# Last sums of the expert outputs: five pairs of tiles on TensorE, three on VectorE, none on GpSimd

## The chip, the cores and the metric

The kernel runs on one core of a Trainium2 chip. The metric is the device time of one execution in microseconds (us). Before the change it was 656.49 us, the median of three runs (655.33 to 656.53).

## What is computed

One transformer layer on 2 x 1024 tokens of width 256, in float32: a modulated layer norm, causal attention with 16 heads, a gated residual, a second modulated layer norm, and a mixture of 16 experts with a shared expert, gated and added to the residual. Only the end matters here. Cut to it, the reference is

```python
w, eidx = jax.lax.top_k(masked, K)            # K = 4 experts of each token
w = w / (w.sum(-1, keepdims=True) + 1e-20)
for e in range(E):                            # cw[:, e] is w where e was chosen, else 0
    a = _swiglu(xt @ expert_up_w[e].T)
    out = out + cw[:, e:e + 1] * (a @ expert_down_w[e].T)
out = out + _swiglu(xt @ shared_up_w.T) @ shared_down_w.T
x = x + gb * out                              # gb: one row for each of the two sequences
```

So each token has four expert outputs. They are weighted with four numbers of the token, summed, multiplied with the row `gb` and added to `x`.

## The kernel before

The 2048 tokens are 16 tiles of 128 (`NT`), one token in each SBUF partition. `X` holds the residual stream, [128, 16, 256].

Attention fills the span up to about 430 us, then the shared expert runs, and from about 460 us on the expert blocks. There are `NB` = 79 blocks of 128 token rows. For a block, SyncE loads the rows into `G`; TensorE turns them (L2376), multiplies with the expert's up weights (L2422), turns the activations (L2434) and multiplies with the down weights (L2446 to L2451); ScalarE and VectorE do the splits in a high and a low part and the SwiGLU between these steps; ScalarE copies the result to `Y` (L1458); GpSimd scatters `Y` to the DRAM tensor `expert_rows` (L1248), so that the four outputs of a token lie beside each other. One step of this loop takes about 2 us.

ScalarE has one more piece of work in this loop. `make_diagonal(i)` (L1466) writes a 128 x 128 diagonal matrix into `DG`, with the weights of one tile's tokens for one of their four experts on the diagonal. It makes one in each step from step `DIAG_FROM` = 12 on, 32 in all.

The expert weights lie in SBUF in 18 slots (`W`, slot k at `k * EW`). Slots 0 and 1 hold the shared expert (`NSH` = 2), slot 2 the first expert. When their contents are no longer needed, the slots are used again: `DG` begins at slot 0, and `Z`, the place for the expert outputs, at slot 2.

When the last needed scatter has landed, the end begins. SyncE issues 16 loads `Z[:, t]` of 512 KB each (L680), one for a tile, and after them, on the same queue, the stores of `X` to `out` (L1030), by pairs of tiles in `STORE_ORDER`. Each of the eight pairs of tiles is summed in one of two ways:

- A pair of `PE_PAIRS`: for each tile TensorE multiplies the four `DG` matrices with the four parts of `Z` and adds them up in PSUM (L2469, `add_outputs`; the trace has eight matrix instructions for a tile). Then VectorE multiplies the sums with the gate row (L2003) and adds them to `X` (L2005): `finish`. The last pair, 7, is finished tile by tile, which halves the size of these instructions.
- Any other pair: ScalarE scales the eight parts of `Z` in place (L1473, `scale_outputs`). Then VectorE or GpSimd does four elementwise instructions, `add_pair`: an addition of 1024 elements in a partition (L723), one of 512 (L725), the product with the gate row (L727) and the addition to `X` (L729). All their operands are in SBUF, while L2003 reads its sums from PSUM.

The division is a constant:

```python
PE_PAIRS, POOL_PAIRS, DVE_PAIRS = (1, 3, 5, 7), (0, 4), (2, 6)
```

Every engine takes its pairs in rising order; VectorE takes 1, 2, 3, 5, 6 and 7. GpSimd's two pairs come after its last scatter.

Of the kernel before, what the change touches and what calls it, by code (L numbers as in the profile page):

```python
# [5 lines left out]
F32 = mybir.dt.float32  # L6
# [5 lines left out]
ALU = mybir.AluOpType  # L12
# [3 lines left out]
P = 128  # L16
B, S, H = 2, 1024, 256
NH, HD = 16, 16
T = B * S
KH = H // P  # L20
NT = T // P
CH = 512
NC = T // CH
# [12 lines left out]
NGR, TOPG, TOPK = 4, 2, 4  # L36
# [9 lines left out]
EW = 2 * HIW + H  # L46
RAW = HIW + H

NSH = 2
# [6 lines left out]
NW = NSH + NE  # L56
# [243 lines left out]
PLACE = [0, 1, 2, 3, 4, 5, 6, 13, 16, 17, 7, 14, 15, 8, 9, 10, 11, 12]  # L300
# [12 lines left out]
COUNT_AT = 8  # L313


PE_PAIRS, POOL_PAIRS, DVE_PAIRS = (1, 3, 5, 7), (0, 4), (2, 6)
SCALED = sorted(POOL_PAIRS + DVE_PAIRS)
LAST_PAIR = NT // 2 - 1
assert LAST_PAIR in PE_PAIRS and sorted(PE_PAIRS + POOL_PAIRS + DVE_PAIRS) == list(range(NT // 2))
ADD_STEPS = 4  # L320

STORE_ORDER = (1, 2, 0, 3, 5, 4, 6, 7)
DIAG_FROM = 12
SP_LOAD, SP_AHEAD = 4, 6


# [3 lines left out]
def program(nc, x, wqk, bqk, wv, bv, wout, bout, cT, wmod, wgate, wsh, wexp, qkd, modrows, hTd, xd, padd, zd, wd, out):  # L330
    with ExitStack() as ctx:

        def sem(name):
            return ctx.enter_context(nc.semaphore(name))
# [19 lines left out]
        X = keep.put("X", [P, NT, H], F32)  # L354
# [33 lines left out]
        att0 = BASE + KEEP + ROWSZ  # L388
# [69 lines left out]
        hv = under.put("hv", [P, KH, CH], F32)  # L458
        SBr = under.put("SBr", [P, B, H], F32)
        CBr = under.put("CBr", [P, B, H], F32)  # L460
        Z = nc.alloc_sbuf_tensor_at("Z", [P, NT, TOPK, H], F32, offset=att0 + NSH * EW * 4)
        assert NSH * EW + NT * TOPK * H <= PLACE[NW - 1] * EW

        DG = nc.alloc_sbuf_tensor_at("DG", [P, 2 * len(PE_PAIRS), TOPK, P], F32, offset=att0)
        assert 2 * len(PE_PAIRS) * TOPK * P <= NSH * EW

        late = Area(att0 + NW * EW * 4, early0 + EARLY - att0 - NW * EW * 4)

# [72 lines left out]
        modrow_in = sem("modrow_in")  # L541
# [96 lines left out]
        x_add = sem("x_add")  # L638
        diag_done = sem("diag_done")
        z_scaled = sem("z_scaled")  # L640
        z_ps = sem("z_ps")
        z_step = sem("z_step")
        z_pool = sem("z_pool")
        fin_done = sem("fin_done")
        out_done = sem("out_done")

# [31 lines left out]
        def load_outputs(queue, t):  # L678

            queue.dma_start(Z[:, t, :, :], zd[t * P * TOPK:(t + 1) * P * TOPK, :].rearrange("(p j) h -> p j h", j=TOPK)  # L680
                            ).then_inc(z_in[t], 16)
# [17 lines left out]
        def pad_experts(queue, which, lo, hi):  # L699

            queue.wait_ge(prow_ready, 1)
            queue.wait_ge(pad_kept, 16 * 4)
            _, first = nc.values_load_multi_w_load_instructions(
                prow[0:1, lo:hi], engines=(which,), min_val=0, max_val=NE * STR - P,
                skip_runtime_bounds_check_because="an expert's stretch has room for every token and the rows behind")
            for e in range(lo, hi):
                queue.dma_start(xd[bass.ds(first[e - lo], P), :], padd[e]).then_inc(pad_out, 16)

        def sums_of(i, first, n):

            if PE_PAIRS[i] == LAST_PAIR:
                return allb[i + first][:, 0:H].unsqueeze(1)
            return allb[i][:, first * H:(first + n) * H].rearrange("p (t h) -> p t h", h=H)

        def gate_of(k):

            return GBr[:, 2 * k // (NT // B), :].unsqueeze(1).broadcast_to([P, 2, H])

        def add_pair(eng, ops, step, i, k):

            z, two = Z[:, 2 * k:2 * k + 2, :, :], slice(2 * k, 2 * k + 2)
            eng.wait_ge(z_scaled, SCALED.index(k) + 1)
            ops.tensor_tensor(z[:, :, 0:2, :], z[:, :, 0:2, :], z[:, :, 2:4, :], ALU.add).then_inc(step, 1)  # L723
            eng.wait_ge(step, ADD_STEPS * i + 1)
            ops.tensor_tensor(z[:, :, 0, :], z[:, :, 0, :], z[:, :, 1, :], ALU.add).then_inc(step, 1)  # L725
            eng.wait_ge(step, ADD_STEPS * i + 2)
            ops.tensor_tensor(z[:, :, 0, :], z[:, :, 0, :], gate_of(k), ALU.mult).then_inc(step, 1)  # L727
            eng.wait_ge(step, ADD_STEPS * i + 3)
            ops.tensor_tensor(X[:, two, :], X[:, two, :], z[:, :, 0, :], ALU.add).then_inc(step, 1)  # L729

        def low_part(eng, ops, c):

# [43 lines left out]
        def _(sp):  # L776
# [240 lines left out]
                sp.wait_ge(y_sc[i], sends[i])  # L1017
            for t in range(NT):
                load_outputs(sp, t)
            for k in STORE_ORDER:  # L1020
                if k in POOL_PAIRS:
                    sp.wait_ge(z_pool, ADD_STEPS * (POOL_PAIRS.index(k) + 1))
                elif k in DVE_PAIRS:
                    sp.wait_ge(z_step, ADD_STEPS * (DVE_PAIRS.index(k) + 1))

                tiles = [(2 * k, 2)] if k != LAST_PAIR else [(2 * k, 1), (2 * k + 1, 1)]
                for t, n in tiles:
                    if k in PE_PAIRS:
                        sp.wait_ge(fin_done, PE_PAIRS.index(k) + 1 + t % 2)
                    sp.dma_start(out[t * P:(t + n) * P, :].rearrange("(t p) h -> p t h", p=P),  # L1030
                                 X[:, t:t + n, :]).then_inc(out_done, 16)
# [6 lines left out]
        def _(pool):  # L1038
# [33 lines left out]
            for k in range(tiles + 1):  # L1072
                if k < tiles:
                    c, i, m = S // CH + k // 4, k % 4, M_ORDER[k % 4]
# [169 lines left out]
            def scatter_block(b):  # L1244

                pool.wait_ge(y_read, b + 1)
                pool.wait_ge(yix_step, 2 * b + 2)
                nc.gpsimd.indirect_dma_start(  # L1248
                    out=zd, out_offset=bass.IndirectOffsetOnAxis(ap=YIX[:, b:b + 1], axis=0),
                    in_=Y[b % YRING], in_offset=None).then_inc(y_sc[b % YRING], 16)  # L1250

            for s in range(NB + 2):
                if s >= 2:
                    scatter_block(s - 2)
            pool.wait_ge(modrow_in, 48)
            pool.wait_ge(x_add, 2 * NC)
            for i, k in enumerate(POOL_PAIRS):
                add_pair(pool, nc.gpsimd, z_pool, i, k)

# [1 line left out]
        def _(act):  # L1263
# [187 lines left out]
            def copy_block(u):  # L1451
                act.wait_ge(y_ps, u + 1)
                if u >= YRING:
                    act.wait_ge(y_sc[u % YRING], 16 * (u // YRING))
                elif u % 2 == 0:

                    act.wait_ge(x_add, 2 * NC - 1 + u // 2)
                nc.scalar.activation(Y[u % YRING], ybank[:, 0:H], ACT.Copy).then_inc(y_read, 1)  # L1458

            def make_diagonal(i):  # L1460

                t, j = 2 * PE_PAIRS[i // (2 * TOPK)] + i // TOPK % 2, i % TOPK
                if i == 0:
                    act.wait_ge(s_down, 2 * NC)
                    act.wait_ge(route_step, NC * ROUTE_STEPS)
                nc.scalar.activation(DG[:, i // TOPK, j, :], ident[:, :], ACT.Identity,  # L1466
                                     scale=W4[:, t, j:j + 1]).then_inc(diag_done, 1)

            def scale_outputs(t):

                act.wait_ge(z_in[t], z_count(t))
                for j in range(TOPK):
                    ins = nc.scalar.activation(Z[:, t, j, :], Z[:, t, j, :], ACT.Identity, scale=W4[:, t, j:j + 1])  # L1473
                return ins

            for s in range(-2, NB + 2):
# [6 lines left out]
                if s >= 2:  # L1483
                    copy_block(s - 2)
                if 0 <= s - DIAG_FROM < 2 * len(PE_PAIRS) * TOPK:
                    make_diagonal(s - DIAG_FROM)
            for k in SCALED:
                for t in (2 * k, 2 * k + 1):
                    ins = scale_outputs(t)
                ins.then_inc(z_scaled, 1)  # L1490
# [3 lines left out]
        def _(dve):  # L1494
# [496 lines left out]
            def act_low(u):  # L1991
                dve.wait_ge(ah_done, u + 1)
                if u >= 2:
                    dve.wait_ge(y_ps, u - 1)
                nc.vector.tensor_tensor(al[u % 2][:, :], abank[:, 0:2 * P], ah[u % 2][:, :].bitcast(F32),
                                        ALU.subtract).then_inc(al_done, 1)

            def finish(i, first, n):

                k = PE_PAIRS[i]  # L2000
                t = slice(2 * k + first, 2 * k + first + n)
                dve.wait_ge(z_ps, 2 * i + first + n)
                nc.vector.tensor_tensor(Z[:, t, 0, :], sums_of(i, first, n), gate_of(k)[:, 0:n, :], ALU.mult).then_inc(s_gated, 1)  # L2003
                dve.wait_ge(s_gated, 2 * NC + i + first + 1)
                nc.vector.tensor_tensor(X[:, t, :], X[:, t, :], Z[:, t, 0, :], ALU.add).then_inc(fin_done, 1)  # L2005

# [10 lines left out]
                    count_sends()  # L2017
            for k in range(NT // 2):
                if k in DVE_PAIRS:
                    add_pair(dve, nc.vector, z_step, DVE_PAIRS.index(k), k)  # L2020
                if k in PE_PAIRS and k != LAST_PAIR:
                    finish(PE_PAIRS.index(k), 0, 2)
            for first in range(2):
                finish(PE_PAIRS.index(LAST_PAIR), first, 1)

        @block.tensor
        def _(pe):
# [435 lines left out]
            def add_outputs(i, u):  # L2463
# [4 lines left out]
                for j in range(TOPK):  # L2468
                    ins = nc.tensor.matmul(sums_of(i, u, 1)[:, 0, :], DG[:, 2 * i + u, j, :], Z[:, t, j, :],  # L2469
                                           start=(j == 0), stop=(j == TOPK - 1))  # L2470
# [64 lines left out]
```

## Time and profile before

| | |
|---|---|
| median of three runs | 656.49 us |
| the profiled execution: device time | 657.58 us |
| the profiled execution: span of the trace | 655.5 us |
| TensorE busy | 583.3 us (89%) |
| VectorE busy | 493.2 us (75%) |
| ScalarE busy | 384.0 us (59%) |
| GpSimd busy | 354.3 us (54%) |
| first load of Z issued | 616.25 us |
| last matrix instruction ends | 645.19 us |
| last instruction of VectorE ends | 650.91 us |

Times in the trace are counted from the start of the span. PE is TensorE, DVE VectorE, ACT ScalarE, POOL GpSimd, SP SyncE; SPq is SyncE's queue of DMA issues. A row of a timeline gives start, duration, engine, line, operation, output and inputs, and in brackets how long the engine was idle before and what it waited for. Between the last instruction of VectorE and the end of the span lie the last store and the end of the program.

### The profile page before, as it was taken

To read this page: it belongs to the slowest core of one execution; us is meant where nothing else is said; L and a number is where in the kernel's file an instruction comes from. 1 tells how busy PE (TensorE), PEld (TensorE's weight loads), DVE (VectorE), ACT (ScalarE), POOL (GpSimd) and SP (SyncE) were. 2 spreads that over 40 slices of the span, in tenths; PEclk is the share of its full clock that TensorE was granted. 3 is DMA by queue.
4 is the path that set the end of the run, shared out by engine and by line. 5 is a ranking of instruction groups with operands and counts; after the bars stand their busy time and mean duration, and the time that the engine had idled before them with its cause. 6 is when DMAs were issued, how large, how long until landed. Compare 5 with 4: busy or idle time off the path is not lost. (4 is left out here: it accounts for less than half of the span.)

```text
span 655.5 us, 13633 instructions
## 1 busy us (share of the span) xinstructions
PE 583.3 (89%) x3944; PEld 394.8 (60%) x3944; DVE 493.2 (75%) x1409; ACT 384.0 (59%) x926; POOL 354.3 (54%) x593
## 2 busy tenths in 40 slices
PE   3979889999999999998987699995999999999972
PEld 3767433434343443444332288774899999999962
DVE  4888978888888769777948657886767777666667
ACT  4547337666667656655857453543367777666671
POOL 5515514455757536854648876772144444444474
PEclk9989969999999999998989989999899999999997
DMA  8359956861707263542215143686954444444594
GB/s 277 125 179 285 350 169 180 209 204 73 233 6 234 86 195 131 168 176 69 82 49 179 51 171 106 232 256 233 342 172 132 134 138 138 133 134 133 187 409 175
DMA packets 69066, 113.62 MB, mean 173 GB/s; under 512 B 12578, under 2 KB 51106, under 8 KB 67844
## 3 DMA queue, kind: packets, MB, share of 16 engines
q1 hardware_dynamic: 62036, 93.74, 44.6%
q0 software_dynamic: 6864, 19.01, 7.5%
q8 instruction: 34, 0.56, 0.4%
q14 instruction: 36, 0.29, 0.1%
q10 hardware_dynamic: 96, 0.01, 0.0%
HBM read 60.57 MB, written 49.94 MB: 169 GB/s over the span
## 5 line engine op out<-in xcount | busy, mean ns | idle before, releaser
L1396 ACT ACTIVATE Pr<-bank 128x512 f32<-128x512 f32 (+3 forms) x384 | 165.8, 494 | 98.3 <-PE bank L2173 93.9
L1248 POOL DMA_INDIRECT expert_rows<-Y,YIX x79 | 75.7, 959 | 104.4 <-DVE ytmp L1957 74.5
L1536 DVE TENSOR_REDUCE mxA<-bank 128x1 f32<-128x128 f32 (+3 forms) x256 | 112.3, 483 | 25.0 <-PE bank L2069 24.8
L2173 PE MATMUL bank<-Qs,Ks 99*128 99x512 bf16 (+3 forms) x384 | 119.5, 336 | 7.4 <-ACT Pr L1396 3.8
L2069 PE MATMUL bank<-Ks,Qs 96*128 96x512 bf16 (+3 forms) x384 | 122.7, 336 | 1.9 <-DVE mxA L1536 1.3
L1536 DVE TENSOR_REDUCE mxB<-bank 128x1 f32<-128x512 f32 x128 | 81.5, 680 | 13.6 <-PE bank L2069 13.6
L2159 PE MATMUL bank<-Pr,Vst 128*32 128x512 f32 (+3 forms) x768 | 84.0, 510 | 5.5 <-POOL Pr L1232 5.3
L1182 POOL DMA_INDIRECT chosen_rows<-Hx,pos x64 | 70.5, 1101 | 22.1 <-issue 17.5
L1230 POOL TENSOR_TENSOR tick<-ident 128x1 f32<-128x1 f32 x128 | 25.3, 198 | 101.5 <-ACT Pr L1396 100.8
L2422 PE MATMUL bank<-W,xh 128*128 x316 | 78.7, 331 | 0.6 <-issue 0.6
L2173 PEld LDWEIGHTS bank<-Qs,Ks 99*128 99x128 bf16 x384 | 36.0, 99 | 61.3 <-ACT Pr L1396 36.6
L2067 PE MATMUL bank<-mask,identb 128*128 128x128 bf16 x256 | 55.3, 228 | 7.6 <-DVE mxA L1536 5.3
L1987 DVE TENSOR_TENSOR act_a<-bank,sg 128x176 f32<-128x176 f32 x79 | 27.0, 341 | 45.8 <-ACT sg L1443 45.8
L2069 PEld LDWEIGHTS bank<-Ks,Qs 96*128 96x128 bf16 x384 | 38.2, 100 | 28.9 <-DVE mxA L1536 5.7
L1232 POOL TENSOR_SCALAR_AFFINE_SELECT Pr<-Pr 128x256 f32<-128x256 f32 x128 | 54.1, 422 | 0.0
L2422 PEld LDWEIGHTS bank<-W,xh 128*128 128x128 f32 x316 | 52.5, 190 | 1.4 <-issue 1.0
L2422 PE MATMUL bank<-W,xl 128*128 x158 | 51.5, 326 | 0.0
L1443 ACT ACTIVATE sg<-bank 128x176 f32<-128x176 f32 x79 | 25.1, 317 | 40.3 <-PE bank L2422 40.3
L2067 PEld LDWEIGHTS bank<-mask,identb 128*128 128x128 bf16 x256 | 25.2, 99 | 30.3 <-DVE mxA L1536 13.8
L1458 ACT ACTIVATE Y<-bank 128x256 f32<-128x256 f32 x79 | 30.4, 384 | 13.8 <-PE bank L2451 4.8
L1950 DVE TENSOR_TENSOR xl<-bank,xh 128x256 fp32r<-128x256 f32 x79 | 32.7, 413 | 5.9 <-ACT xh L1437 5.9
L2376 PE MATMUL bank<-ident,G 128*128 128x128 f32 x158 | 30.9, 278 | 5.4 <-DMA G<-chosen_rows 5.4
(258 smaller groups left out, 1333.0 us busy)
## 6 DMA issues: line engine op xcount, KB each, us to landing
G<-chosen_rows SPq DMA_DIRECT2D x79, 132.0 KB
Z<-expert_rows SPq DMA_DIRECT2D x16, 512.0 KB, 13.5
W<-expert_words SPq DMA_DIRECT2D x7, 1088.0 KB, 6.9
qk_parts<-AP SPq DMA_DIRECT2D x16, 384.0 KB, 5.2
Qs<-qk_parts SPq DMA_DIRECT2D x16, 384.0 KB, 4.6
Ks<-qk_parts SPq DMA_DIRECT2D x8, 768.0 KB, 9.1
Wraw<-in_wexp SPq DMA_DIRECT2D x9, 608.0 KB, 5.7
SA<-in_wexp SPq DMA_DIRECT2D x7, 608.0 KB, 10.8
```

What stands on the lines that cost most here:

```text
L1182: nc.gpsimd.indirect_dma_start(out=xd, out_offset=bass.IndirectOffsetOnAxis(ap=pos[:, c * TPC + t, j:j + 1], axis=0), in_=chosen(c)[:, t, ...
L1232: nc.gpsimd.affine_select(out=v, in_=v, compare_op=ALU.is_ge, fill=0.0, base=0, pattern=[[0, 2], [1, P]], channel_multiplier=-1).then_inc( ...
L1248: nc.gpsimd.indirect_dma_start(out=zd, out_offset=bass.IndirectOffsetOnAxis(ap=YIX[:, b:b + 1], axis=0), in_=Y[b % YRING], in_offset=None) ...
L1396: nc.scalar.activation(Pr[(2 * s + j // 2) % 4][:, j % 2, 0:w], ebank[p % RING][:, 0:w], ACT.Exp, scale=SCALE).then_inc(exp_done, EXP)
L1536: nc.vector.tensor_reduce(dst, mbank[u % RING][:, 0:w], AX.X, ALU.max).then_inc(m_red, 1)
L1950: nc.vector.tensor_tensor(xl[u % 2][:, :], xbank[:, 0:H], xh[u % 2][:, :].bitcast(F32), ALU.subtract).then_inc(xl_done, 1)
L2067: nc.tensor.matmul(mbank[u % RING][:, w - P:w], identb[:, :], mask[:, :], start=True, stop=False, skip_group_check=True)
L2069: nc.tensor.matmul(mbank[u % RING][:, 0:w], Qs[slot][0:NPR, i // TPC, j, (i % TPC) * P:(i % TPC + 1) * P], Ks[slot][0:NPR, j, k0:k0 + w], ...
L2159: ins = nc.tensor.matmul(pvb[32 * j:32 * j + 32, q0:CH], Vst[slot][:, kt, 32 * j:32 * j + 32], Pr[(2 * s + j // 2) % 4][:, j % 2, 0:w], st ...
L2173: nc.tensor.matmul(ebank[p % RING][:, 0:CH - q0], Ks[slot][0:NAUG, j, kt * P:(kt + 1) * P], Qs[slot][0:NAUG, qc, j, q0:CH], start=True, st ...
L2376: ins = nc.tensor.transpose(xbank[:, k * P:(k + 1) * P], G[u % GRING][:, k * P:(k + 1) * P], ident[:, :])
L2422: ins = nc.tensor.matmul(ubank[u % 2][:, 0:2 * EI], x_part[u % 2][:, k * P:(k + 1) * P], words(u, first + k * 2 * EI, 2 * EI), start=(k == ...
```

## The change

GpSimd's two pairs go away. TensorE takes the pairs 0, 2, 4, 6 and 7, VectorE 1, 3 and 5. The stores are issued in rising order. There are 40 diagonals instead of 32; `DG` grows into the slot of the first expert, so `Z` begins one slot later, and the first diagonal is made in step 20, so that the first expert's at most 16 blocks are done before a diagonal is written into its slot. ScalarE scales three pairs instead of four. `add_pair` has the same four instructions, on VectorE alone.

```diff
-PE_PAIRS, POOL_PAIRS, DVE_PAIRS = (1, 3, 5, 7), (0, 4), (2, 6)
-SCALED = sorted(POOL_PAIRS + DVE_PAIRS)
+PE_PAIRS, DVE_PAIRS = (0, 2, 4, 6, 7), (1, 3, 5)
...
-STORE_ORDER = (1, 2, 0, 3, 5, 4, 6, 7)
-DIAG_FROM = 12
+DIAG_FROM = 20
+assert DIAG_FROM >= T // P + 2
...
-        Z = nc.alloc_sbuf_tensor_at("Z", [P, NT, TOPK, H], F32, offset=att0 + NSH * EW * 4)
+        Z = nc.alloc_sbuf_tensor_at("Z", [P, NT, TOPK, H], F32, offset=att0 + (NSH + 1) * EW * 4)
...
-        assert 2 * len(PE_PAIRS) * TOPK * P <= NSH * EW
+        assert 2 * len(PE_PAIRS) * TOPK * P <= (NSH + 1) * EW and PLACE[NSH] == NSH
...
-            for k in STORE_ORDER:
-                if k in POOL_PAIRS:
-                    sp.wait_ge(z_pool, ADD_STEPS * (POOL_PAIRS.index(k) + 1))
-                elif k in DVE_PAIRS:
+            for k in range(NT // 2):
+                if k in DVE_PAIRS:
                     sp.wait_ge(z_step, ADD_STEPS * (DVE_PAIRS.index(k) + 1))
...
-            pool.wait_ge(modrow_in, 48)
-            pool.wait_ge(x_add, 2 * NC)
-            for i, k in enumerate(POOL_PAIRS):
-                add_pair(pool, nc.gpsimd, z_pool, i, k)
...
-            for k in SCALED:
+            for k in DVE_PAIRS:
                 for t in (2 * k, 2 * k + 1):
                     ins = scale_outputs(t)
                 ins.then_inc(z_scaled, 1)
```

## Rows read from the trace of the kernel before

**Rows 1.** The page: busy time of each engine, share and instructions

```profile
PE 583.3 (89%) x3944; PEld 394.8 (60%) x3944; DVE 493.2 (75%) x1409; ACT 384.0 (59%) x926; POOL 354.3 (54%) x593
```

**Rows 2.** The chain that ended last: start, duration, engine and line

```profile
627.01 6.38 ACT Z L1473 x16
633.42 2.07 DVE Z L723
...
650.49 0.42 DVE X L2005
```

**Rows 3.** Timeline of VectorE at the end

```profile
629.75 0.69 DVE L2003 TENSOR_TENSOR Z<-bank,GBr 128x512 f32<-128x512 f32 x1 [4.82 <-PE bank L2469]
...
635.51 1.64 DVE L725 TENSOR_TENSOR Z<-Z 128x512 f32<-128x512 f32 x1
...
643.20 0.68 DVE L2003 TENSOR_TENSOR Z<-bank,GBr 128x512 f32<-128x512 f32 x1
643.91 1.05 DVE L2005 TENSOR_TENSOR X<-X,Z 128x512 f32<-128x512 f32 x1
644.88 2.28 DVE L723 TENSOR_TENSOR Z<-Z 128x1024 f32<-128x1024 f32 x1
647.19 0.69 DVE L725 TENSOR_TENSOR Z<-Z 128x512 f32<-128x512 f32 x1
...
649.25 0.41 DVE L2003 TENSOR_TENSOR Z<-bank,GBr 128x256 f32<-128x256 f32 x1
...
650.04 0.42 DVE L2003 TENSOR_TENSOR Z<-bank,GBr 128x256 f32<-128x256 f32 x1
```

**Rows 4.** Timeline of GpSimd in the same stretch

```profile
634.47 2.13 POOL L727 TENSOR_TENSOR Z<-Z,GBr 128x512 f32<-128x512 f32 x1
...
642.80 1.60 POOL L727 TENSOR_TENSOR Z<-Z,GBr 128x512 f32<-128x512 f32 x1
644.48 1.59 POOL L729 TENSOR_TENSOR X<-X,Z 128x512 f32<-128x512 f32 x1
```

**Rows 5.** VectorE groups by form: count, busy us, mean ns

```profile
L1852 DVE TENSOR_TENSOR SX<-SX,XH 128x1024 fp32r<-128x1024 f32 x4 | 4.9, 1214 | 0.3 <-ACT XH L1363 0.3
```

**Rows 6.** Timeline of TensorE at the end

```profile
626.10 3.62 PE L2469 MATMUL bank<-Z,DG 128*128 128x256 f32 x16
631.24 3.72 PE L2469 MATMUL bank<-Z,DG 128*128 128x256 f32 x16 [1.53 <-DMA Z<-expert_rows]
...
641.47 3.72 PE L2469 MATMUL bank<-Z,DG 128*128 128x256 f32 x16 [1.22 <-DMA Z<-expert_rows]
```

**Rows 7.** Timeline of ScalarE at the end

```profile
634.02 3.30 ACT L1473 ACTIVATE Z<-Z,W 128x256 f32<-128x256 f32 x8 [0.64 <-DMA Z<-expert_rows]
638.97 3.30 ACT L1473 ACTIVATE Z<-Z,W 128x256 f32<-128x256 f32 x8 [1.65 <-DMA Z<-expert_rows]
```

**Rows 8.** Stretches: us, busy PE, PEld, DVE, ACT, POOL, granted clock, DMA share, GB/s

```profile
540.00:550.00 10.00, 10.00 (x77) 9.90 (x76) 6.93 (x31) 7.67 (x26) 4.71 (x6) 1.00 0.43 136
560.00:570.00 10.00, 10.00 (x76) 9.80 (x75) 6.87 (x30) 6.08 (x21) 4.26 (x6) 1.00 0.43 133
```

**Rows 9.** The instructions that write DG: duration min/median/max ns, first and last start

```profile
L1466 ACT ACTIVATE DG<-ident,W x32: 392/392/395, 490.3 to 552.8; 128x128 f32<-128x128 f32 x32
```

**Rows 10.** Store issues from 633 to 634 us: count, KB, us to landing

```profile
out<-X SPq DMA_DIRECT2D x1, 256.0 KB, 10.1
```

**Rows 11.** DMA from 641.0 to 655.5 us: GB/s in 40 slices; last stores

```profile
GB/s 381 206 68 20 260 342 350 345 209 345 333 23 0 175 347 201 138 356 229 0 0 0 0 0 0 147 347 328 263 57 302 3 0 0 0 0 0 0 0 0
...
out<-X SPq DMA_DIRECT2D x2, 128.0 KB, 1.7
```

**Rows 12.** Stretches, columns of Rows 8: a stretch with low clock, the end

```profile
456.00:463.00 7.00, 5.24 (x19) 4.75 (x20) 2.75 (x8) 0.77 (x2) 0.00 (x0) 0.53 0.93 351
...
636.00:641.00 5.00, 3.72 (x16) 2.96 (x16) 4.93 (x3) 3.35 (x10) 4.92 (x3) 1.00 1.02 416
```

**Rows 13.** Timeline of TensorE where the clock is low

```profile
457.76 0.69 PE L2376 MATMUL bank<-ident,G 128*128 128x128 f32 x2 [4.76 <-DMA G<-chosen_rows]
```

More of the change, by code:

```diff
@@ L313 @@
 COUNT_AT = 8
-PE_PAIRS, POOL_PAIRS, DVE_PAIRS = (1, 3, 5, 7), (0, 4), (2, 6)
-SCALED = sorted(POOL_PAIRS + DVE_PAIRS)
+PE_PAIRS, DVE_PAIRS = (0, 2, 4, 6, 7), (1, 3, 5)
 LAST_PAIR = NT // 2 - 1
-assert LAST_PAIR in PE_PAIRS and sorted(PE_PAIRS + POOL_PAIRS + DVE_PAIRS) == list(range(NT // 2))
+assert LAST_PAIR in PE_PAIRS and sorted(PE_PAIRS + DVE_PAIRS) == list(range(NT // 2))
 ADD_STEPS = 4
-STORE_ORDER = (1, 2, 0, 3, 5, 4, 6, 7)
-DIAG_FROM = 12
+DIAG_FROM = 20
+assert DIAG_FROM >= T // P + 2
 SP_LOAD, SP_AHEAD = 4, 6
@@ L460, in program @@
         CBr = under.put("CBr", [P, B, H], F32)
-        Z = nc.alloc_sbuf_tensor_at("Z", [P, NT, TOPK, H], F32, offset=att0 + NSH * EW * 4)
-        assert NSH * EW + NT * TOPK * H <= PLACE[NW - 1] * EW
+        Z = nc.alloc_sbuf_tensor_at("Z", [P, NT, TOPK, H], F32, offset=att0 + (NSH + 1) * EW * 4)
+        assert (NSH + 1) * EW + NT * TOPK * H <= PLACE[NW - 1] * EW
         DG = nc.alloc_sbuf_tensor_at("DG", [P, 2 * len(PE_PAIRS), TOPK, P], F32, offset=att0)
-        assert 2 * len(PE_PAIRS) * TOPK * P <= NSH * EW
+        assert 2 * len(PE_PAIRS) * TOPK * P <= (NSH + 1) * EW and PLACE[NSH] == NSH
         late = Area(att0 + NW * EW * 4, early0 + EARLY - att0 - NW * EW * 4)
@@ L642, in program @@
         z_step = sem("z_step")
-        z_pool = sem("z_pool")
         fin_done = sem("fin_done")
@@ L717, in gate_of @@
             return GBr[:, 2 * k // (NT // B), :].unsqueeze(1).broadcast_to([P, 2, H])
[L719 to L729, printed above, removed]
         def low_part(eng, ops, c):
@@ L1996, in act_low, with add_pair @@
                                         ALU.subtract).then_inc(al_done, 1)
+            def add_pair(i, k):
+                z, two = Z[:, 2 * k:2 * k + 2, :, :], slice(2 * k, 2 * k + 2)
+                dve.wait_ge(z_scaled, DVE_PAIRS.index(k) + 1)
+                nc.vector.tensor_tensor(z[:, :, 0:2, :], z[:, :, 0:2, :], z[:, :, 2:4, :], ALU.add).then_inc(z_step, 1)
+                dve.wait_ge(z_step, ADD_STEPS * i + 1)
+                nc.vector.tensor_tensor(z[:, :, 0, :], z[:, :, 0, :], z[:, :, 1, :], ALU.add).then_inc(z_step, 1)
+                dve.wait_ge(z_step, ADD_STEPS * i + 2)
+                nc.vector.tensor_tensor(z[:, :, 0, :], z[:, :, 0, :], gate_of(k), ALU.mult).then_inc(z_step, 1)
+                dve.wait_ge(z_step, ADD_STEPS * i + 3)
+                nc.vector.tensor_tensor(X[:, two, :], X[:, two, :], z[:, :, 0, :], ALU.add).then_inc(z_step, 1)
             def finish(i, first, n):
@@ L2019, in _ @@
                 if k in DVE_PAIRS:
-                    add_pair(dve, nc.vector, z_step, DVE_PAIRS.index(k), k)
+                    add_pair(DVE_PAIRS.index(k), k)
                 if k in PE_PAIRS and k != LAST_PAIR:
```

## The prediction

> **What bounds the kernel now.** I began with the busy times of the page [rows 1]: TensorE is busy 89% of the span. That says where most of the time goes, not what the change touches. So I took the chain that ended last, from its end backwards [rows 2]. In the last 17 us before VectorE's last instruction, at 650.91 us, the chain is VectorE alone, from 633.42 us on; before that it goes over ScalarE's scaling. TensorE's last matrix instruction ends at 641.47 + 3.72 = 645.19 us [rows 6], 5.7 us earlier. So the end belongs to VectorE, and TensorE's part there has room: it is idle 1.2 to 1.6 us before each of its last three pairs, each time for a load of Z [rows 6]; the rows show the first and the last of these waits.
>
> Then I laid the timelines of VectorE and GpSimd side by side [rows 3, 4]. L725 at 635.51 lasts 1.64 us and ends at 637.15; GpSimd's L727 ends at 636.60, 0.55 us before. L2005 at 643.91 ends at 644.96; GpSimd's L727 ends at 644.40, 0.56 us before. L723 at 644.88 (1024 elements) ends at 647.16; GpSimd's last instruction ends at 644.48 + 1.59 = 646.07 us, 1.09 us before. Once GpSimd is done, an instruction like the first two takes 0.69 us (L725 at 647.19). L2003, which reads one operand from PSUM, takes 0.68 us also beside GpSimd (643.20). The reading: a VectorE instruction with both operands in SBUF stands still until GpSimd's current instruction is over, and then needs its own half microsecond. Eight such instructions lie beside GpSimd's between 630 and 647 us, the three above among them, and each ends 0.54 to 0.56 us (the two of 1024 elements 1.09 us) after the end of a GpSimd instruction. So GpSimd does two pairs and makes VectorE wait for them.
>
> **The change, part by part.** Times are those of the profiled execution; the sum is made on its span of 655.5 us.
>
> *Loads of Z.* They stay. TensorE waits until tile 6 lands at 631.24 and tile 14 at 641.47 us [rows 6], ScalarE for tile 8 until 634.02 and tile 12 until 638.97 us [rows 7]. Eight tiles in 10.23 us are one every 1.28 us, four in 4.95 us one every 1.24: tile 4 is there at about 628.7, tile 5 at 630.0, tile 10 at 636.5, tile 15 at 642.7 us. That Z lies one slot further changes no count and no size, so it has no reason to gain or to lose; I take zero.
>
> *TensorE.* A pair costs 3.62 to 3.72 us [rows 6]. Pair 0 can start at 626.10 as pair 1 does now, and ends at 629.72. Pair 2 (tiles 4 and 5) follows at once, to 633.44. Pair 4 waits for tile 8 until 634.02 and ends at 637.74. Pair 6 waits for tile 12 until 638.97 and ends at 642.69. Pair 7's tile 14 is there since 641.47, so pair 7 follows at once: tile 14 ends at 644.55, tile 15 at 642.69 + 3.72 = 646.41 us. TensorE ends 1.2 us later than now.
>
> *ScalarE.* Three pairs in place of four. A pair takes 3.3 us [rows 7]: pair 1 from 627.0 [rows 2] to 630.3, pair 3 from 631.24 to 634.5, pair 5 from 636.52 to 639.8 us.
>
> *VectorE.* Without GpSimd every instruction has its unblocked length. Finish of a pair: L2003 starts 0.71 us before L2005 (643.20 and 643.91), L2005 takes 0.69 us as L725 does: 1.40 us. add_pair: L725, L727 and L729 at 0.69 us each and 0.03 us between them, 2.14 us; the next L2003 starts 2.06 us behind L725 [rows 3]. L723 alone isn't shown. Its bounds: 2.28 us with 1.19 us beside GpSimd, so at least 1.09 us of its own [rows 3, 4]; at most 1.24 us, the 1.214 us of the form with 1024 elements elsewhere [rows 5] and a start gap. I take 1.24, sum 3.38 us. The last pair, tile by tile, takes 650.91 - 649.25 = 1.66 us. In order: VectorE starts at 629.75; pair 0 ends at 631.15, pair 1 at 634.53, pair 2 at 635.93, pair 3 at 639.31, pair 4 at 640.71, pair 5 at 644.09, pair 6 at 645.49. Each input is there before its turn by the two paragraphs above (the closest are pair 4, 637.74, and pair 5, 639.8). The two tiles of pair 7 would end at 647.15 us; but tile 15's sum comes at 646.41 and its two instructions take 650.91 - 650.04 = 0.87 us, so the end is 647.3 us. TensorE and VectorE are then equally late, within 0.2 us. Now it is 650.91: a gain of 3.6 us.
>
> As a cross-check: GpSimd's blocking costs VectorE some 8.6 us (the excess of the eight instructions over their own length), and the change adds one finish and one add_pair, 4.8 us. The difference is 3.8 us, of which the wait for tile 15 takes 0.1 to 0.2. The bounds of an unblocked L723, three times 1.09 to 1.24 us, move VectorE's end by at most 0.45 us, all of it below TensorE's.
>
> *Stores.* The first store was issued at 633.3 us and landed 10.1 us later [rows 10], behind the loads: the queue serves them in order, so stores issued early take nothing from the loads. In the new kernel the stores of pairs 0 to 4 (1.3 MB) wait behind the loads until about 641.4 us. When the DMA engines are full of stores they move about 345 GB/s [rows 11], so these need 3.8 us, to 645.2; pair 5's, issued at 644.1, is through by about 646.2, pair 6's by 647.6. The last store is issued at 647.3 us and lands after 1.7 us as now [rows 11]. I take no delay. If instead they move at the mean of the eleven slices from 642.5 to 646.4 us, 248 GB/s, 2.1 MB need 8.5 us from 641.4 and end at 649.9, against 649.0 us: up to 0.9 us. SyncE's order is now VectorE's order, so no store waits behind a later one.
>
> *Diagonals.* Eight more on ScalarE, at 0.39 us each [rows 9]. With them the loop's TensorE is busy 10.00 of 10 us, and without them too [rows 8]; ScalarE has 2.3 us of 10 free with them. 31 steps took 62.5 us with diagonals (490.3 to 552.8), 2.02 us each, and without them TensorE does the same count of instructions in 10 us, 76 and 77 [rows 8]. Cover: ScalarE's wait for L2422. I take zero; without cover it is 8 x 0.39 = 3.1 us. Starting in step 20 moves them into equal steps and ends them in step 59 of 79. GpSimd loses only work behind its last scatter.
>
> *Sum.* 655.5 - 3.6 = 651.9 us of span, 654.0 us of device time for an execution like the profiled one (657.58), and 652.9 us on the median of 656.49.
>
> **A rule beside it.** The trace shows VectorE held until GpSimd's instruction ends, and L2003 not held [rows 3, 4]; beside the loads alone it shows no instruction with both operands in SBUF. The Trainium skill, page "SBUF — State Buffer", section "Who interferes with whom", has it that only the port pair of VectorE and GpSimd contends, as an exclusive lock, and that DMA traffic does not slow the engines; by that rule the blocking is gone with GpSimd, the first rival below falls away, and what the trace can show agrees (0.54 to 0.56 us behind GpSimd's ends).
>
> **Rivals.** *The loads slow VectorE, not GpSimd* (slower). Its long instructions mostly lie where loads run. If each instruction with both operands in SBUF costs 0.95 us more until 641.4 us (L725 beside loads and GpSimd took 1.64 [rows 3]), pair 0 ends at 632.1, pair 1 at 639.3, pair 2 at 641.6, and the rest, 3.38 + 1.41 + 3.38 + 1.41 + 1.66, at 652.8: 1.9 us slower, 658.4. It decides as soon as the cost per instruction passes about 0.6 us. Against it: L2005 at 643.91 is long after the loads, and the ends follow GpSimd's. Chance 0.04.
>
> *The clock falls in the end* (slower). At 457.76 TensorE had been idle 4.76 us and the stretch had a granted clock of 0.53, so mostly the 1.2 GHz level [rows 12, 13]. If the wait for tile 12 in the end did that, pairs 6 and 7 would take twice 3.72 us each and end at 653.9, VectorE at 654.7: 3.8 us slower, 660.3. It decides if more than one pair runs at 1.2 GHz. Against it: with idle times up to 1.6 us the clock is 1.00 now [rows 6, 12], and the new waits are at most 1.23 us. The Trainium skill, page "TensorE: Matmul & The Clock Gate", section "HAM oscillation — how this bites in real kernels", tells of kernels whose bursts between DMA waits each start at the low clock; the trace does not show that for waits of this length. Chance 0.04.
>
> *The diagonals cost their full time.* 3.1 us of the 3.6 are lost, 656.0 us. Against it are the equal steps. Chance 0.06.
>
> *The stores set the end.* 0.9 us of delay, 653.8 us. Chance 0.10.
>
> **How the numbers follow.** The forecast, 652.9 us, has a chance of 0.76; its own scatter is that of the runs, 655.33 to 656.53, less 3.6 to 3.8: 651.5 to 652.9, and a few tenths above for gaps on VectorE, which now has no idle time to hide any. With the stores' case and up to 0.8 us of them on a bad run the range is 651.7 to 654.6 us; it leaves out the cases with 0.14. A measurement of this kernel can tell about 0.2% (1.3 us) from no change. Faster: 0.76 + 0.10, less 0.01 for a bad sum: 0.85. Within 0.2%: 0.07. Slower: 0.08.
>
> **What would show it.** In the new profile: L2003, L2005 and L725 to L729 at 0.69 us, L723 at 1.1 to 1.2 us, no VectorE idle time from 629.8 to 645.5 us; five TensorE groups of 3.7 us that end near 646.4; the chain's end going from a matrix instruction of pair 7 to L2003; stores landing behind the loads; a block step still 2.01 us. The prediction is wrong if VectorE's instructions stay above 1 us without GpSimd, if the granted clock is below 1.00 before 646 us, or if the last store lands more than 2 us after its issue.

## The result, and the profile after

The changed kernel takes 650.44 us (median of 9 runs, 646.99 to 653.67) where the kernel before takes 656.49 us. The ratio is 0.9884, with a 95% interval from 0.9860 to 0.9908: 7.6 us faster (6.0 to 9.2). I had forecast 652.9 us with a range from 651.7 to 654.6, so the sign was right, the time lies below the range and the gain was more than twice the forecast 3.6 us. (The 7.6 us go by the ratio; the two medians differ by 6.05 us, which is at the low end of its interval.) Measured twice more, beside the experiments, it was 0.9866 (0.9821 to 0.9911) and 0.9898 (0.9863 to 0.9934).

Single executions of either kernel differ by several microseconds (652.24 to 659.95 for the kernel before), and the profiled ones are such executions: the first load of Z is issued at 616.25 us in the trace of before and at 612.00 us in that of after. So times of the end are counted from the first load of Z from here on, which takes what lies ahead out of the comparison. Two of the experiments below (the late GpSimd instruction and the fills) have a profiled execution that was slow ahead of this stretch; of these, too, only the stretch is read.

VectorE's timeline of the changed kernel, for [rows 3]. L1996 and L1998 are the former L2003 and L2005, L1983 to L1989 the former L723 to L729:

```profile
625.43 0.69 DVE L1996 TENSOR_TENSOR Z<-bank,GBr 128x512 f32<-128x512 f32 x1 [4.84 <-PE bank L2462]
626.16 0.69 DVE L1998 TENSOR_TENSOR X<-X,Z 128x512 f32<-128x512 f32 x1
626.77 1.22 DVE L1983 TENSOR_TENSOR Z<-Z 128x1024 f32<-128x1024 f32 x1
628.02 0.69 DVE L1985 TENSOR_TENSOR Z<-Z 128x512 f32<-128x512 f32 x1
628.75 0.69 DVE L1987 TENSOR_TENSOR Z<-Z,GBr 128x512 f32<-128x512 f32 x1
629.47 0.69 DVE L1989 TENSOR_TENSOR X<-X,Z 128x512 f32<-128x512 f32 x1
630.08 0.68 DVE L1996 TENSOR_TENSOR Z<-bank,GBr 128x512 f32<-128x512 f32 x1
...
640.69 0.42 DVE L1996 TENSOR_TENSOR Z<-bank,GBr 128x256 f32<-128x256 f32 x1
641.14 0.43 DVE L1998 TENSOR_TENSOR X<-X,Z 128x256 f32<-128x256 f32 x1
641.48 0.42 DVE L1996 TENSOR_TENSOR Z<-bank,GBr 128x256 f32<-128x256 f32 x1
641.94 0.42 DVE L1998 TENSOR_TENSOR X<-X,Z 128x256 f32<-128x256 f32 x1
```

Nothing is held any more, though the loads run as before: 0.69 us where L725 took 1.64 [rows 3], 1.22 where L723 took 2.28. After the first one, no instruction has an idle time before it. VectorE ends at 642.36 us, 30.4 us after the first load; before it was 650.91, 34.7 us after it.

TensorE and ScalarE, for [rows 6] and [rows 7]. L2462 is the former L2469, L1454 the former L1473; a group of 32 is two pairs without a pause:

```profile
621.78 7.07 PE L2462 MATMUL bank<-Z,DG 128*128 128x256 f32 x32
629.23 3.72 PE L2462 MATMUL bank<-Z,DG 128*128 128x256 f32 x16 [0.38 <-DMA Z<-expert_rows]
634.19 7.17 PE L2462 MATMUL bank<-Z,DG 128*128 128x256 f32 x32 [1.24 <-DMA Z<-expert_rows]
```

```profile
631.68 3.30 ACT L1454 ACTIVATE Z<-Z,W 128x256 f32<-128x256 f32 x8 [1.96 <-DMA Z<-expert_rows]
```

TensorE ends at 641.36 us, 1.0 us ahead of VectorE. The granted clock is 1.00 throughout (two stretches for [rows 12]; columns as in [rows 8]), and the first store, for [rows 10], still lands behind the loads. The last stores, for [rows 11], take 1.7 us as before:

```profile
625.00:630.00 5.00, 4.62 (x22) 3.74 (x21) 4.43 (x6) 4.14 (x11) 0.00 (x0) 1.00 1.03 419
...
635.00:640.00 5.00, 5.00 (x25) 4.41 (x24) 4.86 (x7) 0.00 (x0) 0.00 (x0) 1.00 1.01 369
```

```profile
out<-X SPq DMA_DIRECT2D x1, 256.0 KB, 11.0
```

```profile
out<-X SPq DMA_DIRECT2D x2, 128.0 KB, 1.7
```

The diagonals, for [rows 9]: 40 in 78.6 us are 39 steps of 2.02 us, against 2.02 before. No cost of theirs shows.

```profile
L1447 ACT ACTIVATE DG<-ident,W x40: 392/392/394, 502.1 to 580.7; 128x128 f32<-128x128 f32 x40
```

All this accounts for VectorE's 4.3 us. The rest is behind VectorE's last instruction: to the end of the span it is 655.47 - 650.91 = 4.6 us in the trace of before and 644.59 - 642.36 = 2.2 us in that of after. The list of what SyncE's queue waited for in the end shows where (us in total, times, longest). Before:

```profile
SPq L331 <- PEq L331: 2.5, 1, 2.5
...
SPq L1035 <- DMA out<-X: 1.3, 1, 1.3
```

After:

```profile
SPq L1020 <- DMA out<-X: 1.3, 1, 1.3
SPq L331 <- PEq L331: 0.2, 1, 0.2
```

L1035 and L1020 are the wait for the last store: equal. L331 is the line that holds the whole program, and the wait recorded there is the meeting of all engines at its end. The list names TensorE's sequencer, which had long been done. The trace's own records, below the level of the page, have the engine that came last: GpSimd closes its program with an instruction that the records call DRAIN, after which it reports to the others. It ends at 655.24 us in the kernel before, 9.2 us after the end of GpSimd's last addition and 2.6 us after SyncE had seen the last store; the other engines are released 0.2 us later. In the changed kernel GpSimd's last instruction is a scatter that ends at 623.89, its DRAIN ends at 633.62, and nobody waits for it.

### The profile page after: what moved, and what is told of

Same layout as the page of the kernel before. It is cut to its first block and busy times, and to the rows that moved or that the text cites. A ratio compares the mean times of both kernels' runs of the same rounds, so it can differ in the third digit from the quotient of the medians.

```text
span 644.6 us, 13664 instructions
## 1 busy us (share of the span) xinstructions
PE 582.1 (90%) x3960; PEld 395.7 (61%) x3960; DVE 487.5 (76%) x1415; ACT 382.8 (59%) x926; POOL 337.9 (52%) x585
## 5 line engine op out<-in xcount | busy, mean ns | idle before, releaser
L2060 PEld LDWEIGHTS bank<-mask,identb 128*128 128x128 bf16 x256 | 25.1, 98 | 30.0 <-DVE mxA L1517 13.6
L1439 ACT ACTIVATE Y<-bank 128x256 f32<-128x256 f32 x79 | 30.3, 384 | 13.7 <-PE bank L2444 5.4
```

The source lines that it names most:

```text
L2060: nc.tensor.matmul(mbank[u % RING][:, w - P:w], identb[:, :], mask[:, :], start=True, stop=False, skip_group_check=True)
```

## The experiments

All numbers in this table are from the profiled executions but the ratio, which is that of the timed runs to the kernel before on the same chip, with its interval. "VectorE" and "span" are the ends of VectorE's last instruction and of the span, in us after the first load of Z.

| kernel | VectorE | span | ratio |
|---|---|---|---|
| before | 34.7 | 39.2 | |
| before, again | 34.3 | 38.8 | 1.0005 (0.9967 to 1.0043) |
| before, later diagonals, Z moved | 35.1 | 39.7 | 1.0002 (0.9979 to 1.0024) |
| after | 30.4 | 32.6 | 0.9884 (0.9860 to 0.9908) |
| after, again | 30.5 | 32.7 | 0.9866 (0.9821 to 0.9911) |
| after, third time | 30.6 | 32.8 | 0.9898 (0.9863 to 0.9934) |
| four pairs on each of TensorE and VectorE | 32.5 | 34.7 | 0.9921 (0.9886 to 0.9957) |
| before, GpSimd's sums left out | 31.2 | 33.4 | 0.9905 (0.9871 to 0.9939) |
| before, one pair on GpSimd | 34.2 | 36.4 | 0.9979 (0.9944 to 1.0014) |
| after, five reads on GpSimd | 34.9 | 37.1 | 0.9959 (0.9923 to 0.9994) |
| after, five fills on GpSimd | 30.3 | 32.5 | 0.9879 (0.9806 to 0.9951) |
| after, one late instruction on GpSimd | 30.3 | 38.9 | 1.0000 (0.9959 to 1.0041) |

**The kernel before, unchanged.**

> The kernel before, unchanged, against itself: it measures the scatter, in time and in where the stretch ahead of the end lies. In the two profiles so far the first load of Z is issued at 616.25 us (before) and 612.00 us (after), though the code ahead of it is the same but for the place and the step of the diagonals. Theory (only the end changed; the 4.2 us ahead of the first load are scatter of single executions): ratio 1.000 within 0.3%, and over the profiles of all runs here the first load lies anywhere between 611 and 617 us, for kernels with and without the change. Rival (the changed layout speeds the part ahead of the first load): the kernels that have the old layout have their first load near 616 us, those with the new one near 612 us. Both expect here a span that ends 39.2 us after the first load, as in the profile of before (655.47 - 616.25), and VectorE's last instruction 34.7 us after it.

The ratio is 1.0005, the stretch 38.8 us. Its first load lay at 627.3 us, outside the 611 to 617 us that were expected. Over all profiles the kernels with the old layout have theirs at 616.3, 626.2, 626.9 and 627.3 us, those with the new one at 612.0, 614.5, 616.7, 625.3, 627.5, 631.6, 633.3 and 637.7 us. The chips differ, and so do single executions; the new layout's are not all the earlier ones. So the profiles give no clear sign of a gain ahead of the end; whether the 4.2 us between the first two are scatter is for the timed runs of the last experiment to say.

**Four pairs each, none on GpSimd.**

> The changed kernel, but with the pairs 1, 3, 5, 7 on TensorE and 0, 2, 4, 6 on VectorE: GpSimd is taken out of the end, and no fifth pair is given to TensorE. Times from the first load of Z on. Theory (the gain comes from taking GpSimd out: VectorE is no longer held, and GpSimd's last instruction no longer sets the end of the program): four add_pairs at 3.31 us, three finishes at 1.34, the last pair 1.67 us are 18.9 us of VectorE from 14.0 us on, so VectorE ends at 32.9 us (before 34.7, after 30.4) and the span at 35.1 us (before 39.2, after 32.6): 4.1 us faster than before, 652.4 us, two thirds of the whole gain. Rival (what counts is the fifth pair on TensorE, VectorE's own work being the bound either way): VectorE ends at 34.7 us or later and the time is that of before within 1 us.

```diff
-PE_PAIRS, DVE_PAIRS = (0, 2, 4, 6, 7), (1, 3, 5)
+PE_PAIRS, DVE_PAIRS = (1, 3, 5, 7), (0, 2, 4, 6)
```

VectorE ends at 32.5 us and the span at 34.7, 0.4 us below what was expected (VectorE starts 13.6 us after the first load, not 14.0), and 4.1 to 5.0 us below the three profiles in which GpSimd has two pairs. So most of the gain comes with GpSimd's leaving, not with the fifth pair on TensorE. The fifth pair brings the other 2.0 us, the difference of an add_pair and a finish (3.31 - 1.34).

**GpSimd's sums left out.**

> The kernel before with GpSimd's two add_pairs left out (the sums of the pairs 0 and 4 are missing from the output; their loads, scalings and stores stay). TensorE and VectorE keep their pairs. It measures what GpSimd's work costs the others. Theory (GpSimd holds VectorE's instructions): L2005 and L725 to L729 take 0.69 us each and L723 1.21 us at all times; VectorE then waits for its inputs (pair 5 until 24.0 us after the first load, pair 6 until 26.1) and ends 31.1 us after the first load of Z in place of 34.7, the span at 33.3 in place of 39.2: 5.9 us faster, 650.6 us. Rival (the loads hold VectorE): instructions with both operands in SBUF take 1.6 us or more as long as loads run, and VectorE ends at 33 us or later.

```diff
-            pool.wait_ge(modrow_in, 48)
-            pool.wait_ge(x_add, 2 * NC)
-            for i, k in enumerate(POOL_PAIRS):
-                add_pair(pool, nc.gpsimd, z_pool, i, k)
...
-                    sp.wait_ge(z_pool, ADD_STEPS * (POOL_PAIRS.index(k) + 1))
+                    sp.wait_ge(x_add, 2 * NC)
```

VectorE's timeline; L1999 and L2001 are L2003 and L2005 of before, the pairs as in [rows 3]:

```profile
640.53 0.69 DVE L2001 TENSOR_TENSOR X<-X,Z 128x512 f32<-128x512 f32 x1
643.29 1.23 DVE L723 TENSOR_TENSOR Z<-Z 128x1024 f32<-128x1024 f32 x1 [2.06 <-ACT Z L1469]
644.54 0.69 DVE L725 TENSOR_TENSOR Z<-Z 128x512 f32<-128x512 f32 x1
...
651.07 0.69 DVE L1999 TENSOR_TENSOR Z<-bank,GBr 128x512 f32<-128x512 f32 x1 [3.06 <-PE bank L2465]
```

Every instruction has its short length while the loads run, and VectorE idles 2.06 and 3.06 us for its inputs. The expected 31.1 and 33.3 us came out as 31.2 and 33.4. The rival that the loads slow VectorE is gone.

**One late instruction on GpSimd.**

> The changed kernel with one tiny instruction (128x1) on GpSimd that waits until TensorE has made all its sums, 29.4 us after the first load of Z. The traces show that the span of before ends 9.4 us after GpSimd's last instruction (646.07 to 655.47), though the last store had landed at 652.6 us; in the changed kernel it ends 20.7 us after GpSimd's last instruction and 0.5 us after the last store. Theory (after its last instruction GpSimd needs 9.2 to 9.7 us to come to its end, whatever that instruction was, and the program ends with the last engine): the span ends at 29.6 + 9.4 = 39.0 us after the first load instead of 32.6, so 6.4 us later than the changed kernel, a time about like that of before. Rival (the time after GpSimd's last instruction was the store or the size of the work): no change against the changed kernel.

```diff
             for s in range(NB + 2):
                 if s >= 2:
                     scatter_block(s - 2)
+            pool.wait_ge(z_ps, 2 * len(PE_PAIRS))
+            nc.gpsimd.tensor_tensor(tick[:, 0:1], ident[:, 0:1], ident[:, 0:1], ALU.mult)
```

The timeline and SyncE's wait at the end of the program:

```profile
666.89 0.40 POOL L1241 TENSOR_TENSOR tick<-ident 128x1 f32<-128x1 f32 x1 [17.48 <-PE bank L2464]
667.15 0.41 DVE L1998 TENSOR_TENSOR Z<-bank,GBr 128x256 f32<-128x256 f32 x1
667.60 0.42 DVE L2000 TENSOR_TENSOR X<-X,Z 128x256 f32<-128x256 f32 x1
```

```profile
SPq L331 <- PEq L331: 6.6, 1, 6.6
```

One element in each partition, 0.40 us of work beside everything else, and the span ends at 676.66 us, 8.6 us after VectorE's last instruction: 38.9 us after the first load where 39.0 was expected. That is 6.3 us later than the changed kernel, and the ratio to the kernel before is 1.0000 (0.9959 to 1.0041): within that interval this one instruction gives back the whole gain, with VectorE as early as in the changed kernel. It decides for the time that GpSimd needs to come to its end, and against the stores and the size of the work. GpSimd's ends, from the trace's records of its last instruction and its DRAIN (its closing instruction):

```
kernel                      last instruction     ends      drain ends   difference
before                      L729, 512 elements   646.07    655.24       9.2
one pair on GpSimd          L729, 512 elements   648.94    658.11       9.2
five reads                  512 elements         655.06    664.22       9.2
five fills                  1536 elements        653.55    662.69       9.1
late instruction            1 element            667.29    676.43       9.1
after                       scatter              623.89    633.62       9.7
after, third time           scatter              628.63    638.49       9.9
four pairs each             scatter              639.11    648.72       9.6
GpSimd's sums left out      scatter              638.12    647.86       9.7
```

**One pair on GpSimd.**

> The kernel before with pair 4 moved from GpSimd to VectorE; pair 0 stays on GpSimd, the pairs 1, 3, 5, 7 on TensorE. It parts the two costs of GpSimd. GpSimd's last instruction now ends 22 us after the first load of Z, so that its end of program, 9.2 us on, lies at 31 us and bounds nothing; VectorE is still held until 22 us and has one add_pair more. Theory: VectorE ends where it did, 34.2 us after the first load (three add_pairs and four finishes from 13.5 us on with some 4 us of being held), and the span ends 2.2 us after it, at 36.5 us in place of 38.8 to 39.2: 2.3 to 2.7 us faster than before, all of it GpSimd's end of program. Rival (the time behind VectorE's last instruction belongs to the stores): the span ends 4.6 us after VectorE again, and nothing is gained.

```diff
-PE_PAIRS, POOL_PAIRS, DVE_PAIRS = (1, 3, 5, 7), (0, 4), (2, 6)
+PE_PAIRS, POOL_PAIRS, DVE_PAIRS = (1, 3, 5, 7), (0,), (2, 4, 6)
```

VectorE ends at 34.2 us, where it did, and the span at 36.4 us: the two costs come apart as expected, to 0.1 us. SyncE's wait at L331 is 0.2 us. The ratio, 0.9979, has 1.0 in its interval; it agrees with the 2.4 to 3.3 us of the stretch, but doesn't show them by itself.

**Reads and fills on GpSimd.**

> The changed kernel with five instructions added on GpSimd, each an addition of 512 elements in a partition, read from and written to SBUF that is no longer needed; they begin when the first pair is scaled, 13.9 us after the first load of Z, and take 1.6 us each, to 22 us. The end of GpSimd's program lies then at 31.3 us, ahead of the end. Theory (an instruction of VectorE with both operands in SBUF waits until GpSimd's current instruction is over): until 22 us each L2005, L723, L725, L727 and L729 ends 0.55 us (L723 1.1 us) after an end of a GpSimd instruction; VectorE's first add_pair ends near 22.7 us in place of 18.1, so VectorE ends at 34.7 us and the span at 36.9 us, 4.4 us later than the changed kernel. Rival (GpSimd was slow itself and VectorE was slow from the loads or the memory): VectorE's lengths stay at 0.69 and 1.22 us.

```diff
+            pool.wait_ge(y_ps, NB)
+            pool.wait_ge(z_scaled, 1)
+            for i in range(5):
+                nc.gpsimd.tensor_tensor(Wraw[14 + i // 2][:, 512 * (i % 2):512 * (i % 2) + 512].rearrange("p (a n) -> p a n", a=2),
+                                        *(t[:, :].unsqueeze(1).broadcast_to([P, 2, 2 * P]) for t in act_a), ALU.add)
```

```profile
646.45 2.33 DVE L1988 TENSOR_TENSOR Z<-Z 128x1024 f32<-128x1024 f32 x1
648.81 1.68 DVE L1990 TENSOR_TENSOR Z<-Z 128x512 f32<-128x512 f32 x1
650.52 1.67 DVE L1992 TENSOR_TENSOR Z<-Z,GBr 128x512 f32<-128x512 f32 x1
652.23 1.67 DVE L1994 TENSOR_TENSOR X<-X,Z 128x512 f32<-128x512 f32 x1
653.83 0.68 DVE L2001 TENSOR_TENSOR Z<-bank,GBr 128x512 f32<-128x512 f32 x1
654.54 1.07 DVE L2003 TENSOR_TENSOR X<-X,Z 128x512 f32<-128x512 f32 x1
655.54 1.21 DVE L1988 TENSOR_TENSOR Z<-Z 128x1024 f32<-128x1024 f32 x1
```

```profile
645.85 9.21 POOL L1243 TENSOR_TENSOR Wraw<-act_a,act_a 128x512 f32<-128x512 f32 x5 [2.10 <-ACT Z L1459]
```

The five additions bring the long lengths back, and only until they are over at 655.06 us; L2001, with its PSUM operand, keeps its 0.68 us between them. L2003 at 654.54 ends at 655.61 us, 0.55 us after the last addition. The additions took 9.2 us together where 8 was expected. VectorE ends at 34.9 us, 4.5 us later than in the changed kernel, where 34.7 was expected.

> As the kernel with five additions on GpSimd, but with five fills of 1536 elements in a partition, which read nothing and only write (about 1.35 us each by the fill of 3840 elements, 3.33 us). Theory in its narrow form (VectorE waits for GpSimd's reads): VectorE's lengths stay at 0.69 and 1.22 us, and the end does not move. Theory in its wide form (VectorE waits for any instruction of GpSimd that touches SBUF): VectorE's instructions with both operands in SBUF end 0.55 us after ends of the fills until about 21 us, and the end comes 2 to 4 us later.

```diff
+            for i in range(5):
+                nc.gpsimd.memset(W[:, 13 + i, 0:1536].bitcast(F32), 0.0)
```

```profile
646.89 6.65 POOL L1243 MEMSET W<- 128x1536 f32 x5 [2.07 <-ACT Z L1458]
```

```profile
647.99 1.22 DVE L1987 TENSOR_TENSOR Z<-Z 128x1024 f32<-128x1024 f32 x1
649.25 0.69 DVE L1989 TENSOR_TENSOR Z<-Z 128x512 f32<-128x512 f32 x1
```

Beside fills VectorE is not held at all, and the end stays at 32.5 us. The narrow form holds for the two kinds that ran here: VectorE's instructions with two SBUF operands wait for a GpSimd addition, which reads SBUF and writes it, and not for a fill, which only writes. The Trainium skill, page "SBUF — State Buffer", section "Who interferes with whom", draws the same line between GpSimd instructions that read and those that only write; these two runs agree with it.

**What lies ahead of the end.** The changed kernel was measured again beside the experiments.

> The changed kernel once more, beside the experiments. Theory (the gain is that of the stretch from the first load of Z to the end of the span, 39.2 and 38.8 us in the two profiles of the kernel before, 32.6 us in that of the changed one; the part ahead of the first load only scatters): that stretch is 32.6 us again, VectorE's last instruction ends 30.3 us after the first load, and the time is 6.2 to 6.6 us below the kernel before, a ratio of 0.990 to 0.991. Rival (a part of the 4.2 us ahead of the first load belongs to the change): the ratio is 0.986 or less.

The stretch is 32.7 us, as expected, but the ratio, 0.9866, is nearer to the rival; its interval, 0.9821 to 0.9911, holds both. So the changed kernel went to one chip once more, with the kernel before that has only the new placing.

> The changed kernel a third time, for its interval. Theory: the stretch from the first load of Z to the end of the span is 32.6 us, the time 6.1 to 6.6 us below the kernel before, ratio 0.990 to 0.991. Rival (a part of the gain lies ahead of the first load): ratio 0.988 or less again.

> The kernel before with nothing changed but the two things of the change that lie ahead of the end: the diagonals are made from step 20 on instead of 12, and Z lies one slot further. Timed with the changed kernel on one chip, to settle whether a part of the gain lies ahead of the first load of Z. So far the changed kernel's time fell by 7.6 us (interval 6.0 to 9.2) and 9.0 us (6.0 to 12.0), and the stretch from the first load to the end of the span by 6.1 to 6.6 us. Theory (nothing ahead of the first load changed): ratio 1.000 within its interval, stretch from the first load to the end 38.8 to 39.2 us. Rival (the placing brings the rest): ratio 0.996 to 0.998, 1.2 to 2.6 us.

```diff
-DIAG_FROM = 12
+DIAG_FROM = 20
...
-        Z = nc.alloc_sbuf_tensor_at("Z", [P, NT, TOPK, H], F32, offset=att0 + NSH * EW * 4)
+        Z = nc.alloc_sbuf_tensor_at("Z", [P, NT, TOPK, H], F32, offset=att0 + (NSH + 1) * EW * 4)
```

The placing alone gives 1.0002 (0.9979 to 1.0024), nothing; the changed kernel gives 0.9898, or 6.7 us, and 32.8 us of stretch. The rival finds no support. This kernel still makes 32 diagonals; that the eight further ones gain or cost nothing rests on the equal steps.

## Why the prediction was wrong

**Sound: what holds VectorE.** That GpSimd's instructions hold VectorE's, and that 0.69 us and 1.22 us remain without them, came out to 0.02 us, and both ways of it, taking GpSimd's work away and putting it back, were shown by runs.

**Sound: the order of the work.** TensorE's five groups, with waits for the tiles 8 and 12 alone, are the ones of the working. TensorE ended 29.4 us after the first load where 30.2 was worked out: the wait for tile 12 ended 22.2 us after the first load in place of 22.7, and the two pairs behind it took 7.17 us in place of 7.44. Diagonals at no visible cost, stores behind the loads, the clock at 1.00 and 1.7 us for the last store: all as written. None of the four rivals happened.

**Mis-sized: VectorE's sum.** I had 17.55 us from its first sum to its end (629.75 to 647.3); it took 16.93 (625.43 to 642.36). A finish was set at 1.40 us and an add_pair at 3.38; in the timeline above they are 1.34 (625.43 to 626.77) and 3.31 (626.77 to 630.08), because an instruction that reads nothing its predecessor wrote starts some 0.08 us before the predecessor's end. [rows 3] had shown that: the next L2003 starts 2.06 us behind L725, not 2.14, and I quoted it and then summed with 2.14. Four finishes and three add_pairs make 0.45 us of it. The other 0.15 us is the wait for tile 15's sum, which didn't come since TensorE was earlier. In the mean of three profiles each (for before those of before, before again, and before with the new placing), VectorE's end went from 34.7 to 30.45 us, a gain of 4.2 us in place of 3.6. The mechanism was right here, and this term was too small by 0.6 us.

**Failed: the step "655.5 - 3.6".** The sum carried the 4.6 us between VectorE's last instruction and the end of the span over unchanged, as the last store and the end of the program. The remaining 2.9 us, behind the 1.7 us of the store, were never asked for. Of these some 0.5 us come in the changed kernel too (2.2 less 1.7), and 2.3 us were GpSimd's way to its end, 9.2 us long and begun at 646.07. So the kernel before had two ends close together, VectorE's at 653.1 (650.91 + 2.2) and GpSimd's at 655.5, and the later was GpSimd's. A faster VectorE alone would not have moved the span: with one late instruction on GpSimd, VectorE ends at 30.3 us and the span still at 38.9. The chain that ended last did not show it, since it goes back from the last instruction that counts as work, and the DRAIN is not one. "GpSimd loses only work behind its last scatter", I wrote, and gave it no price. The row that should have stopped me was SyncE's 2.5 us at L331, a wait with no work behind it. With 2.3 us more the forecast would have been 650.6 us.

**The sum now.** 4.2 us from VectorE and 2.3 us from GpSimd's end are 6.5 us (39.2 to 32.7 us, means of three profiles each). That lies in all three measured intervals, 6.0 to 9.2, 6.0 to 12.0 and 4.3 to 9.0 us, but at the low end of the first two. Whether another microsecond comes from somewhere else is open: the placing shows none, within 1.6 us, and the difference of the first two medians, 6.05 us, doesn't ask for one.

**A better version.** After the change TensorE's last sum (641.36) and VectorE's turn for it (641.48) meet within 0.12 us, and VectorE has no idle time ahead of it. A fourth pair on VectorE costs 2.0 us (the kernel with four each). A sixth pair on TensorE would add 3.7 us of work there, of which its 1.6 us of waits could cover a part: 2.1 to 3.7 us later, an estimate from its groups. No run tried it.

## What to carry to other kernels

Before a sum is made on a span, account for everything between the last instruction on the critical chain and the span's end. A long wait of SyncE at the program's closing line asks which engine comes to its end late; here it was GpSimd, 9.1 to 9.9 us after its last instruction. In a kernel like this one, let GpSimd's last instruction, however small, end some 10 us before the span does. Beside a VectorE stretch whose operands are all in SBUF, GpSimd's additions and products were not free help: each held VectorE until it was over, while fills held nothing, and VectorE instructions with a PSUM operand passed.

## What the runs showed of the hardware

GpSimd's closing DRAIN ends 9.1 to 9.2 us after an elementwise instruction, whether of 1, 512 or 1536 elements in a partition (late instruction, before, fills), and 9.6 to 9.9 us after a scatter (four pairs each, after). Fills of 1536 elements on GpSimd (1.38 us each) leave VectorE's instructions of 512 elements with two SBUF operands at 0.69 us, while additions of 512 elements stretch them to 1.67 us. DMA traffic of 419 GB/s beside them does not lengthen them: 0.69 us in the changed kernel.
